# A gated recurrence over 16 batches on one core: one batch a pass, and two

## The chip, the core and the metric

The kernel runs on one NeuronCore of a Trainium2 chip. Times are device microseconds (us) of one execution. The engines are PE (TensorE, matmuls), DVE (VectorE), ACT (ScalarE), POOL (GpSimd) and SP (SyncE, which here only issues transfers). A semaphore is what one engine counts up and another waits for.

## What is computed

`x` is 16 x 224 x 512: 16 batches of 224 tokens. Three stages follow each other, each with a residual and a layer norm: self-attention, cross-attention against a 750-token context, and a recurrent block. Only the last one changes. In the kernel's terms its reference is:

```python
def step(c, xt):                       # scanned over the 16 batches, state c is 224 x 512
    ft = sigmoid(xt @ wf.T + c @ uf.T + bf)
    it = sigmoid(xt @ wi.T + c @ ui.T + bi)
    gt = tanh(xt @ wc.T + c @ uc.T + bc)
    return ft * c + it * gt
c_final = scan(step, c0, x)            # c0 is in_c, the same row for all 224 tokens
h = tanh(x @ wo.T + c_final @ uo.T + bo)
```

The scan is serial over the batches. The input products `xt @ w` don't depend on the state.

## The kernel before

`decoder` calls `self_attention`, `cross_attention` and `feed_forward`, the last of which calls `recurrence` and `output_gate`. Each of these parts is a block of its own; a barrier of all engines stands between two of them.

In `recurrence` everything is turned: 512 state rows lie as 4 groups of 128 partitions, the 224 tokens are the columns. Each f32 operand is split into a rounded part and a rest (`_hi`, `_lo`), and a product is three matmuls: hi x hi, lo x hi, hi x lo. With 4 groups of contraction, one output tile (128 rows x 224 columns) costs 12 matmuls.

- PE: `x_turn(b)` turns batch b with 8 transposes into `ps_x`; `x_part(b)` is the input product, 3 gates x 4 row groups = 12 tiles, 144 matmuls of 224 columns into `ps_gate`, where the sums stay open; `c_part(b)` adds the state product, 144 matmuls more, and closes them. `step(b)` is x_part(b), x_turn(b+1), c_part(b). The six banks of `ps_gate` hold one gate of one half (two row groups) each.
- ACT: `xth` rounds the turned x to `xt_hi`; `gates` takes the tanh of each tile straight from `ps_gate` with the bias (a sigmoid is a tanh of half the argument).
- DVE: `xtl` makes `xt_lo`; `state` combines the gates to the new `c` in halves and splits it into `c_hi` and `c_lo`. `cl_done` is what c_part waits for.
- SP: `load(b)` brings x of the next batch, one buffer `x2_raw`. Ahead of that loop SP loads the recurrence's own weights: three (`wf`, `wi`, `wc`) have come into the three `raw` buffers during cross-attention, then `uf`, `ui`, `uc`, `uo`, `wo` follow, each as soon as its buffer has been split. All of a transfer's descriptors are taken in the order of issue.
- The weights' rounding is ACT's and their rest DVE's; `uo` and `wo` (needed only in `output_gate`) are both POOL's.

While the next state is worked out from batch b's gates, PE does x_part(b+1), which needs no state.

## Time and profile before

| | us |
|---|---|
| median of 3 runs (lowest, highest) | 1599.73 (1598.21, 1603.63) |
| the profiled execution: its time, its span | 1605.2, 1603.3 |
| recurrence, from its first product to its last matmul's start group | 935.54 to 1469.21 |
| one step in the steady loop | 33.0 |
| output gate, to the end | 1474.7 to 1603.3 |

The profile's page gives busy time by engine and in 40 equal slices; the granted PE clock stands in tenths of full speed. Matmuls overlap in the pipeline, so the duration of one (275 ns) is not what it costs: the cost is the distance between the starts of neighbours, called the pitch below. Rows of one kind that follow each other are merged in the timeline, with their count (x4).

### The profile page before, as it was taken

Reading aid. Unit: us, or ns where it says so; the run is one execution under the profiler, and the core shown is the slowest. Engines: PE = TensorE matmul, PEld = TensorE weight load, DVE = VectorE, ACT = ScalarE, POOL = GpSimd, SP = SyncE. Lnnn points to the kernel's source line nnn. Section 1 sums busy time; section 2 is a strip of 40 time slices with the busy share of each in tenths; the row PEclk is TensorE's granted clock in tenths of the full one; section 3 lists DMA queues with packets and bytes.
Section 4 is the critical chain, followed back from the end, with each engine's and each line's share of the span. In section 5 each row is a group of like instructions: output and inputs, shape, how many; then the busy total and the mean of one; then the engine's idle time right before and its main releaser. Section 6 shows DMA issues by size and latency. Waiting matters only on the chain. (4 is left out here: it accounts for less than half of the span.)

```text
span 1603.3 us, 32782 instructions
## 1 busy us (share of the span) xinstructions
PE 1515.5 (95%) x12306; PEld 1342.6 (84%) x12306; DVE 807.8 (50%) x1841; ACT 607.4 (38%) x1883; POOL 530.6 (33%) x398
## 2 busy tenths in 40 slices
PE   6999999996899999999999769999999999998996
PEld 3677777774698999999999669999999999998774
DVE  3688888884255666657566342221222212221676
ACT  4777777771244444444444131111111112211221
POOL 2455454542345666656656221000000000000344
PEclk8899999998899999999999879999999999999998
DMA  2253233222336433434433050000000000001343
GB/s 75 59 170 93 84 87 92 78 62 80 111 110 197 148 122 129 161 119 132 147 130 119 12 175 15 11 11 11 23 11 11 11 11 23 11 0 42 102 138 92
DMA packets 70089, 129.03 MB, mean 80 GB/s; under 512 B 6610, under 2 KB 14802, under 8 KB 70036
## 3 DMA queue, kind: packets, MB, share of 16 engines
q1 hardware_dynamic: 70036, 128.33, 25.5%
q8 instruction: 32, 0.52, 0.1%
q14 instruction: 21, 0.17, 0.0%
HBM read 106.30 MB, written 22.02 MB: 80 GB/s over the span
## 5 line engine op out<-in xcount | busy, mean ns | idle before, releaser
L333 ACT ACTIVATE a_p<-a_ps_s,a_nmax 112x224 f32<-112x224 f32 (+1 forms) x512 | 198.3, 416 | 85.8 <-DVE a_nmax L396 85.8
L510 POOL TENSOR_TENSOR a_p<-a_p,a_rinv 112x896 f32<-112x896 f32 (+1 forms) x128 | 164.8, 1308 | 163.4 <-DVE a_rinv L404 158.7
L1543 POOL MEMSET o_mhalf<- 112x2 f32 x1 | 0.1, 99 | 508.3 <-POOLq L1078 508.3
L1241 ACT ACTIVATE f_gate<-f_ps_gate,f_bias 128x224 f32<-128x224 f32 x192 | 75.4, 444 | 195.2 <-PE f_ps_gate L1204 195.2
L1033 POOL TENSOR_TENSOR x_cx_lo<-x_cx_raw,x_cx_hi 125x512 fp32r<-125x512 f32 x96 | 120.5, 1293 | 83.8 <-ACT x_cx_hi L845 83.8
L1027 POOL TENSOR_TENSOR x_ct_lo<-x_ct_raw,x_ct_hi 128x750 fp32r<-128x750 f32 x64 | 117.5, 1865 | 21.3 <-ACT x_ct_hi L819 21.3
L237 PEld LDWEIGHTS a_ps_t<-a_identity,a_p 112*112 112x112 f32 x768 | 88.2, 137 | 32.1 <-POOL a_p L510 10.3
L333 ACT ACTIVATION_READ_ACCUMULATOR a_p<-a_ps_s,a_nmax 112x1 f32 x512 | 113.7, 222 | 0.0
L237 PE MATMUL a_ps_t<-a_identity,a_p 112*112 112x112 f32 x768 | 109.0, 267 | 2.3 <-DVE a_pt L411 2.2
L1275 DVE TENSOR_TENSOR f_xt_lo<-f_ps_x,f_xt_hi 128x448 fp32r<-128x448 f32 x16 | 10.0, 624 | 195.6 <-ACT f_xt_hi L1232 195.6
L395 DVE TENSOR_REDUCE a_nmax<-a_ps_s 112x1 f32<-112x224 f32 x256 | 97.4, 380 | 19.4 <-PE a_ps_s L224 19.2
L411 DVE COPY a_pt<-a_ps_t 112x448 f32<-112x448 f32 x128 | 79.2, 619 | 46.5 <-PE a_ps_t L237 46.5
L1231 ACT ACTIVATE f_xt_hi<-f_ps_x 128x448 fp32r<-128x448 f32 x16 | 8.7, 543 | 235.1 <-PE f_ps_x L1170 235.1
L1286 DVE SCALAR_TENSOR_TENSOR f_fresh<-f_gate 128x448 f32<-128x448 f32 x32 | 20.0, 625 | 146.8 <-ACT f_gate L1241 146.8
L1020 POOL TENSOR_TENSOR x_x1b<-x_x_raw,x_bv_all 112x1024 f32<-112x1024 f32 x16 | 38.3, 2392 | 94.2 <-DVE x_r L948 92.6
L396 DVE TENSOR_REDUCE a_nmax<-a_ps_s 112x1 f32<-112x112 f32 x256 | 67.5, 264 | 0.0
L266 PE MATMUL a_ps_w<-a_w_hi,a_yt_lo 128*112 128x512 f32 x128 | 64.4, 517 | 0.0
L936 DVE TENSOR_REDUCE x_smax<-x_ps_s 112x1 f32<-112x750 f32 x32 | 30.1, 939 | 58.0 <-PE x_ps_s L762 58.0
L748 PE MATMUL x_ps_g<-x_pt_hi,x_cx_hi 125*128 125x224 f32 x384 | 54.8, 280 | 3.2 <-DVE x_pt_lo L914 3.2
L852 ACT ACTIVATE x_p<-x_ps_s,x_shift 112x750 f32<-112x750 f32 x32 | 28.4, 887 | 75.8 <-DVE x_shift L941 75.8
L748 PE MATMUL x_ps_g<-x_pt_hi,x_cx_lo 125*128 125x224 f32 x384 | 54.2, 278 | 0.0
L218 PE MATMUL a_ps_s<-a_xt,a_zs 32*112 32x224 f32 x512 | 51.1, 399 | 3.2 <-DVE a_bu_split L454 2.1
(225 smaller groups left out, 4046.9 us busy)
## 6 DMA issues: line engine op xcount, KB each, us to landing
x_ct_raw<-in_ct SPq DMA_DIRECT2D x16, 1500.0 KB, 7.8
x_cx_raw<-in_cx SPq DMA_DIRECT2D x16, 1500.0 KB
a_xt<-in_xt SPq DMA_DIRECT2D x16, 448.0 KB, 3.9
a_xrow<-in_x SPq DMA_DIRECT2D x16, 448.0 KB, 3.5
a_xres<-in_x SPq DMA_DIRECT2D x16, 448.0 KB, 4.6
x_scratch<-a_xn SPq DMA_DIRECT2D x16, 448.0 KB, 3.2
x_x_raw<-x_scratch SPq DMA_DIRECT2D x16, 448.0 KB, 3.7
x_scratch<-x_xn SPq DMA_DIRECT2D x16, 448.0 KB, 6.2
```

The source lines that it names most:

```text
L218: pe.matmul(ps_s[0:R, h, 0:T], zs[rows, g, R:T], xt[rows, odd, g, :], start=True, stop=False, skip_group_check=True)
L237: mm = pe.transpose(ps_t[0:R, (g + unit) % 2, h * R:h * R + R], src, identity[0:R, 0:R])
L266: mm = pe.matmul(ps_w[0:R, :], *products[i], start=(i == 0), stop=(i == len(products) - 1))
L333: e = act.activation((p1 if c else p0)[:, g, h, :], src, ACT.Exp, bias=nmax[:, g % 2, c, h:h + 1], accum_out=rsum[:, g % 2, c, h:h + 1])
L395: dve.tensor_reduce(nmax[:, g % 2, 1, h:h + 1], ps_s[0:R, h, 0:T], AX.X, ALU.max, negate=True)
L396: dve.tensor_reduce(nmax[:, g % 2, 0, h:h + 1], ps_s[0:R, h, T:T + R], AX.X, ALU.max, negate=True)\
L411: dve.tensor_copy(transposed(g, unit), unit_bank(g, unit)).then_inc(ptd_done, 1)
L510: pool.tensor_tensor(p[:, g, :, :], p[:, g, :, :], inv, ALU.mult).then_inc(norm_done, 1)
L748: mm = pe.matmul(pair(ps_g, dk), v[:, j, 128 * dk:128 * dk + 128], q[:, j, :], start=(i == 0), stop=(i == 3 * XC - 1))
L1027: pool.tensor_tensor(ct_lo[:, k, 0:TX], ct_raw[:, k, :], ct_hi[:, k, 0:TX], ALU.subtract).then_inc(ctl_done, 1)
L1033: pool.tensor_tensor(cx_lo[:, j, :], cx_raw[:, j, :], cx_hi[:, j, :], ALU.subtract).then_inc(cxl_done, 1)
L1241: a = act.activation(gate[:, j, m, :], region(3 * half + j, k2), ACT.Tanh, bias=bias[:, j, m:m + 1], scale=0.5 if j < 2 else 1.0)
```

## The change

Batches are taken in pairs (8 of them). x of both batches of a pair is turned into `xt_hi`/`xt_lo` of 2 x 224 columns, and `x_part(pair, half)` makes 6 of the pair's 12 tiles with 448 columns in one matmul. A tile goes through `ps_x` (two banks in turn); ACT copies it with the bias into SBUF (`xg_early`, `xg_late`), counted by `xg_done`. The state's two parts stand side by side in `cc`, so `c_tile` has 4 matmuls of hi weights over 448 columns (hi x hi and hi x lo at once) and 4 of lo weights over 224. Nothing is summed in PSUM across these: DVE's new `add` takes the first 224 columns plus the stored input product, then the second 224, per gate and half; ACT's tanh then reads `gate` in SBUF, 448 elements at once.

For batch 0 the state is the same column for all tokens: `u_part` multiplies it as one column with the unsplit weights (48 matmuls) in place of 144, and `opening_gates` feeds the result in as a bias. The state is kept doubled, which saves DVE one operation per half. PE's order is now, for a pair: state product of the first batch (with the two turns of the next pair inside), first half of the next pair's input product, state product of the second batch, second half of the input product. In the last pair there is no next input product; the second batch's first half is done in two pieces by contraction group.

POOL splits `wi` and `ui` at the start. `uo` and `wo` now land in the SBUF of `wf` and `wi`: POOL splits them when the last input product is done. SP loads them into `raw` only after `u_done`, since `u_part` reads `raw`; the loads of x for batches 2 and 3 are issued behind them.

```diff
+            load(0, 0)
+            load(1, 1)
...
             for i in range(3, len(plan)):
-                sp.wait_ge(w_split, i - 2)
+                sp.wait_ge(w_split[i - 3], 1)
+                if i >= 6:
+                    sp.wait_ge(u_done, 1)
                 load_weight(sp, raw[i % 3], raw_in[i % 3], plan[i][0])
-            with sp.Fori(1, B) as b:
-                load(b)
+            with sp.Fori(1, B // 2) as i:
+                for a in range(2):
+                    load(2 * i + a, a)
...
+            def split(i):
...
+            split(1)
+            split(4)
+            pool.wait_ge(xpart_done, TILES * (B // 2))
+            split(6)
+            split(7)
...
+            def x_turn(b, a):
+                if not within(b, B):
+                    return
+                wait(pe, x2_in[a], 8 * (b - a) + 16)
+                if a == 0:
+                    wait(pe, xg_done, (TILES // 2) * b)
+                elif not (isinstance(b, int) and b == 1):
+                    wait(pe, xtl_done, b)
...
+            def x_part(pair, half):
...
+                wait(pe, xtl_done, 2 * pair + 2)
...
+                    for k2 in range(HC):
+                        t = 6 * half + 2 * j + k2
+                        m = slice(128 * (HC * half + k2), 128 * (HC * half + k2) + 128)
+                        if t >= 2:
+                            wait(pe, xg_done, TILES * pair + t - 1)
+                        i = 0
+                        for wp, xp in ((0, xt_hi), (1, xt_hi), (0, xt_lo)):
+                            for k in range(KC):
+                                mm = pe.matmul(ps_x[:, t % 2, 0:2 * T], w["w" + n][wp][:, k, m], xp[:, k, :, :],
+                                               start=(i == 0), stop=(i == 3 * KC - 1))
+                                i += 1
+                        mm.then_inc(xpart_done, 1)
+            def u_part():
+                pe.wait_ge(b_in, 64)
+                for j in range(3):
+                    pe.wait_ge(raw_in[j], 16 * 3)
+                    for m in range(KC):
+                        for k in range(KC):
+                            mm = pe.matmul(ps_gate[:, U_BANK, KC * j + m:KC * j + m + 1], raw[j][:, k, 128 * m:128 * m + 128], c0[:, k:k + 1],
+                                           start=(k == 0), stop=(k == KC - 1))
+                mm.then_inc(u_done, 1)
+            def c_tile(half, j, k2, ks):
+                m = slice(128 * (HC * half + k2), 128 * (HC * half + k2) + 128)
+                hi, lo = w["u" + GATES[j]]
+                for k in ks:
+                    pe.matmul(ps_gate[:, 2 * j + k2, 0:2 * T], hi[:, k, m], cc[:, k, :, :], start=(k == 0), stop=False, skip_group_check=True)
+                for k in ks:
+                    mm = pe.matmul(ps_gate[:, 2 * j + k2, 0:T], lo[:, k, m], cc[:, k, 0, :], start=False, stop=(k == KC - 1),
+                                   skip_group_check=True)
+                return mm
+            def c_gate(b, half, j, ks=range(KC)):
+                if ks[0] == 0:
+                    if isinstance(b, int) and b == 1 and half == 0:
+                        pe.wait_ge(w_split[3 + j], 1)
+                        pe.wait_ge(u_bias_done, 3)
+                    wait(pe, add_done, 6 * (b - 1) + 3 * half + j - 2)
+                for k2 in range(HC):
+                    mm = c_tile(half, j, k2, ks)
+                if ks[-1] == KC - 1:
+                    mm.then_inc(gate_done, 1)
+            def pair_steps(i):
...
+                if not (isinstance(i, int) and i == 0):
+                    wait(pe, cl_done, 2 * first)
+                    c_gate(first, 0, 0)
+                x_turn(first + 2, 0)
+                if not (isinstance(i, int) and i == 0):
+                    c_gate(first, 0, 1)
+                    c_gate(first, 0, 2)
+                x_turn(first + 3, 1)
+                if not (isinstance(i, int) and i == 0):
+                    for j in range(3):
+                        c_gate(first, 1, j)
+                x_part(i + 1, 0)
+                if isinstance(i, int) and i == B // 2 - 1:
+                    pe.wait_ge(cl_done, 2 * second - 1)
+                    for j in range(3):
+                        c_gate(second, 0, j, range(0, HC))
+                    pe.wait_ge(cl_done, 2 * second)
+                    for j in range(3):
+                        c_gate(second, 0, j, range(HC, KC))
+                else:
+                    wait(pe, cl_done, 2 * second)
+                    for j in range(3):
+                        c_gate(second, 0, j)
+                for j in range(3):
+                    c_gate(second, 1, j)
+                x_part(i + 1, 1)
+            x_turn(0, 0)
+            x_turn(1, 1)
+            for half in range(2):
+                x_part(0, half)
+            u_part()
+            pair_steps(0)
+            with pe.Fori(1, B // 2 - 2) as i:
+                pair_steps(i)
+            for i in range(B // 2 - 2, B // 2):
+                pair_steps(i)
...
+                wait(act, xpart_done, (TILES // 2) * (b - a))
+                act.activation(xt_hi[:, 0:2, a, :], turned(b, 0), ACT.Copy)
+                act.activation(xt_hi[:, 2:4, a, :], turned(b, 2), ACT.Copy).then_inc(xth_done, 1)
...
+            def opening_gates():
+                act.wait_ge(u_done, 1)
+                for j in range(3):
+                    act.activation(u_bias[:, j, :], ps_gate[:, U_BANK, KC * j:KC * j + KC], ACT.Copy, scale=0.5 if j < 2 else 1.0)\
+                       .then_inc(u_bias_done, 1)
+                act.wait_ge(u_bias_done, 3)
+                act.wait_ge(xg_done, TILES)
                 for half in range(2):
...
-                            a = act.activation(gate[:, j, m, :], region(3 * half + j, k2), ACT.Tanh, bias=bias[:, j, m:m + 1],
+                            a = act.activation(gate[:, j, m, :], pre(0, half, j)[:, k2, 0, :], ACT.Tanh, bias=u_bias[:, j, m:m + 1],
                                                scale=0.5 if j < 2 else 1.0)
                         a.then_inc(act_done, 1)
...
+            def pair_steps(i, odd_pair):
+                if isinstance(i, int) and i == 0:
+                    xth(2, 0)
+                    opening_gates()
+                    xth(3, 1)
+                else:
+                    xth(2 * i + 2, 0)
+                    gate_tanh(2 * i, 0, 0)
+                    gate_tanh(2 * i, 0, 1)
+                    xth(2 * i + 3, 1)
+                    gate_tanh(2 * i, 0, 2)
+                    for j in range(3):
+                        gate_tanh(2 * i, 1, j)
+                x_gates(i + 1, 1 - odd_pair, 0)
+                for half in range(2):
+                    for j in range(3):
+                        gate_tanh(2 * i + 1, half, j)
+                x_gates(i + 1, 1 - odd_pair, 1)
...
+            round_weight(0)
+            xth(0, 0)
+            xth(1, 1)
+            round_weight(2)
+            act.wait_ge(b_in, 64)
+            for j in range(3):
+                x_gate(0, 0, 0, j)
+                if j == 1:
+                    round_weight(3)
+            for j in range(3):
+                x_gate(0, 0, 1, j)
+                if j == 1:
+                    round_weight(5)
+            for i in range(2):
+                pair_steps(i, i)
+            with act.Fori(1, B // 4 - 1) as i:
+                for odd_pair in range(2):
+                    pair_steps(2 * i + odd_pair, odd_pair)
+            for i in range(B // 2 - 2, B // 2):
+                pair_steps(i, i % 2)
...
+            def add(b, odd_pair, a, half, j):
+                cols = slice(HC * half, HC * half + HC)
+                n = 6 * (b - 1) + 3 * half + j
+                wait(dve, gate_done, n + 1)
+                wait(dve, xg_done, 6 * (b - a) + 6 * half + 2 * j + 2)
+                dve.tensor_tensor(gate[:, j, cols, :], ps_gate[:, 2 * j:2 * j + 2, 0:T], pre(odd_pair, half, j)[:, :, a, :],
+                                  ALU.add).then_inc(hi_added, 1)
+                wait(dve, hi_added, n + 1)
+                dve.tensor_tensor(gate[:, j, cols, :], ps_gate[:, 2 * j:2 * j + 2, T:2 * T], gate[:, j, cols, :],
+                                  ALU.add).then_inc(add_done, 1)
...
+                dve.scalar_tensor_tensor(out=state[:, cols, :], in0=kept[:, cols, :], scalar=0.5, in1=fresh[:, cols, :],
+                                         op0=ALU.mult, op1=ALU.add).then_inc(state_done, 1)
...
+                dve.tensor_scalar(cc[:, cols, 0, :], state[:, cols, :], 0.5, None, ALU.mult).then_inc(ch_done, 1)
+                wait(dve, ch_done, n + 1)
+                dve.scalar_tensor_tensor(out=cc[:, cols, 1, :], in0=state[:, cols, :], scalar=0.5, in1=cc[:, cols, 0, :],
+                                         op0=ALU.mult, op1=ALU.subtract).then_inc(cl_done, 1)
+            def second_half(b, odd_pair, a):
+                add(b, odd_pair, a, 1, 0)
+                add(b, odd_pair, a, 1, 1)
+                split(b, 0)
+                add(b, odd_pair, a, 1, 2)
+                cell(b, 1)
+                split(b, 1)
+            def pair_steps(i, odd_pair):
+                if isinstance(i, int) and i == 0:
+                    xtl(2, 0)
+                    cell(0, 0)
+                    split(0, 0)
+                    cell(0, 1)
+                    split(0, 1)
+                    xtl(3, 1)
+                else:
+                    add(2 * i, odd_pair, 0, 0, 0)
+                    xtl(2 * i + 2, 0)
+                    add(2 * i, odd_pair, 0, 0, 1)
+                    add(2 * i, odd_pair, 0, 0, 2)
+                    xtl(2 * i + 3, 1)
+                    cell(2 * i, 0)
+                    second_half(2 * i, odd_pair, 0)
+                for j in range(3):
+                    add(2 * i + 1, odd_pair, 1, 0, j)
+                cell(2 * i + 1, 0)
+                second_half(2 * i + 1, odd_pair, 1)
```

PE in the steady loop of the kernel before, at the seam between the input product of one batch and its state product (the stationary operand is named last):

```order
L1187 MATMUL f_ps_gate<-f_xt_hi,f_wc_hi 128x224 x4
L1187 MATMUL f_ps_gate<-f_xt_hi,f_wc_lo 128x224 x4
L1187 MATMUL f_ps_gate<-f_xt_lo,f_wc_hi 128x224 x4
L1170 MATMUL f_ps_x<-f_identity,f_x_raw 128x112 x8
L1204 MATMUL f_ps_gate<-f_c_hi,f_uf_hi 128x224 x4
L1204 MATMUL f_ps_gate<-f_c_hi,f_uf_lo 128x224 x4
L1204 MATMUL f_ps_gate<-f_c_lo,f_uf_hi 128x224 x4
```

PE in the kernel after, at the top of a pair, where the turn stands between two gates of the first batch's state product:

```order
L1238 MATMUL f_ps_gate<-f_cc,f_uf_hi 128x448 x4
L1240 MATMUL f_ps_gate<-f_cc,f_uf_lo 128x224 x4
L37 ISA
L37 REGISTER_ALU
L1201 MATMUL f_ps_x<-f_identity,f_x_raw 128x112 x8
L37 REGISTER_ALU
L1238 MATMUL f_ps_gate<-f_cc,f_ui_hi 128x448 x4
L1240 MATMUL f_ps_gate<-f_cc,f_ui_lo 128x224 x4
```

Three groups of four matmuls of 224 columns per tile have become one group of four with 448 columns and one with 224.

The second place is the start of the recurrence after the first pair's input product. SP's queue there, before:

```order
L46 DMA w_raw<-in_uf_t 128x4x512 [waits f_w_split]
L46 DMA w_raw<-in_ui_t 128x4x512 [waits f_w_split]
L46 DMA w_raw<-in_uc_t 128x4x512 [waits f_w_split]
L46 DMA w_raw<-in_uo_t 128x4x512 [waits f_w_split]
L46 DMA w_raw<-in_wo_t 128x4x512 [waits f_w_split]
L1143 UNCONDITIONAL_BRANCH
L1132 ISA [waits f_xt_done]
L1132 DMA f_x_raw<-x_scratch 112x2x512
```

and after:

```order
L46 DMA w_raw<-in_uf_t 128x4x512 [waits f_w0_split]
L46 DMA w_raw<-in_ui_t 128x4x512 [waits f_w1_split]
L46 DMA w_raw<-in_uc_t 128x4x512 [waits f_w2_split]
L46 DMA w_raw<-in_uo_t 128x4x512 [waits f_u_done,f_w3_split]
L46 DMA w_raw<-in_wo_t 128x4x512 [waits f_u_done,f_w4_split]
L1162 UNCONDITIONAL_BRANCH
L1162 ISA
L1149 ISA [waits f_xt_done]
L1149 DMA f_x_raw<-x_scratch 112x2x512
```

The loads of `uo`, `wo` and x now stand behind PE's `u_part`. The third place is ACT after the first pair's last input tile, in the kernel after:

```order
L1302 ACTIVATE f_xt_hi<-f_ps_x 128x2x224 [waits f_xpart_done,f_xt_done]
L1303 ACTIVATE f_xt_hi<-f_ps_x 128x2x224
L1328 ACTIVATE f_u_bias<-f_ps_gate 128x4 [waits f_u_done]
L1328 ACTIVATE f_u_bias<-f_ps_gate 128x4 x2
L1336 ACTIVATE f_gate<-f_xg_early,f_u_bias 128x224 [waits f_xg_done,f_u_bias_done]
L1336 ACTIVATE f_gate<-f_xg_early,f_u_bias 128x224 x5
L1336 ACTIVATE f_gate<-f_xg_late,f_u_bias 128x224 x6
L1302 ACTIVATE f_xt_hi<-f_ps_x 128x2x224 [waits f_xpart_done,f_xt_done]
```

The rounding of batch 2's turned x stands ahead of batch 0's gates, that of batch 3 behind them.

## Rows read from the trace of the kernel before

**Rows 1.** The page: PE's busy share and granted clock in 40 equal slices.
```profile
PE   6999999996899999999999769999999999998996
PEclk8899999998899999999999879999999999999998
```

**Rows 2.** Windows: us, then busy (instructions) by engine, clock, DMA share.
```profile
1092.00:1422.00 330.00, 330.00 (x2969) 330.00 (x2967) 75.53 (x140) 57.21 (x141) 0.00 (x0) 1.00 0.05 14
```

**Rows 3.** Timeline, PE, one input product, the turn: start, us, line, tile.
```profile
1075.19 0.61 PE L1187 MATMUL f_ps_gate<-f_xt_hi,f_wf_hi 128*128 128x224 f32 x4
...
1091.27 0.93 PE L1170 MATMUL f_ps_x<-f_identity,f_x_raw 112*128 112x112 f32 x8
...
1091.97 0.69 PE L1204 MATMUL f_ps_gate<-f_c_hi,f_uf_hi 128*128 128x224 f32 x4
```

**Rows 4.** Timeline, PE in cross-attention, 376 and 512 columns.
```profile
704.11 1.52 PE L762 MATMUL x_ps_s<-x_ct_hi,x_zt_hi 128*112 128x376 f32 x8
...
712.31 0.93 PE L716 MATMUL x_ps_g<-x_identity,x_x_raw 112*128 112x112 f32 x8
...
713.99 1.08 PE L774 MATMUL x_ps_h<-x_wv_lo,x_ot_hi 128*112 128x512 f32 x4
...
717.69 1.09 PE L774 MATMUL x_ps_h<-x_wv_hi,x_ot_lo 128*112 128x512 f32 x4
```

**Rows 5.** By line: a product of one column with unsplit weights.
```profile
L703 PEld LDWEIGHTS x_ps_g<-x_bq,w_raw x32: 191/192/193, 413.1 to 416.8; 128*128 128x128 f32 x32
```

**Rows 6.** Timeline, opening of the recurrence, all engines.
```profile
929.03 1.73 PE L1170 MATMUL f_ps_x<-f_identity,f_x_raw 112*128 112x112 f32 x8 [12.15 <-DMA f_x_raw<-x_scratch]
...
935.54 1.20 PE L1187 MATMUL f_ps_gate<-f_xt_hi,f_wf_hi 128*128 128x224 f32 x4 [4.78 <-DVE f_xt_lo L1276]
940.80 0.71 PE L1187 MATMUL f_ps_gate<-f_xt_hi,f_wi_hi 128*128 128x224 f32 x4
...
947.85 0.37 SPq L46 DMA_DIRECT2D w_raw<-in_wo_t  x1
...
957.83 1.57 PE L1170 MATMUL f_ps_x<-f_identity,f_x_raw 112*128 112x112 f32 x8 [3.36 <-DMA f_x_raw<-x_scratch]
```

**Rows 7.** DMA view: transfers, KB each, us from issue to landing.
```profile
w_raw<-in_uf_t SPq DMA_DIRECT2D x1, 1024.0 KB, 5.2
...
w_raw<-in_wo_t SPq DMA_DIRECT2D x1, 1024.0 KB, 8.8
```

**Rows 8.** By tile, the recurrence's x: shortest, median, longest landing.
```profile
DMA to landing us min/median/max: 3.4/3.6/9.3
```

**Rows 9.** Timeline, POOL's split of `wo` and a DVE operation beside it.
```profile
959.79 1.89 POOL L1157 CAST f_wo_hi<-w_raw 128x2048 fp32r<-128x2048 f32 x1
...
961.76 4.58 POOL L1159 TENSOR_TENSOR f_wo_lo<-w_raw,f_wo_hi 128x2048 fp32r<-128x2048 f32 x1
...
964.00 2.82 DVE L1283 SCALAR_TENSOR_TENSOR f_keep<-f_gate,f_c 128x448 f32<-128x448 f32 x1 [2.39 <-ACT f_gate L1241]
```

**Rows 10.** Timeline, the last matmuls of the recurrence and the state's last steps.
```profile
1469.21 0.61 PE L1204 MATMUL f_ps_gate<-f_c_lo,f_uc_hi 128*128 128x224 f32 x4
1469.85 0.78 ACT L1241 ACTIVATE f_gate<-f_ps_gate,f_bias 128x224 f32<-128x224 f32 x2 [1.90 <-PE f_ps_gate L1204]
1470.67 0.62 DVE L1286 SCALAR_TENSOR_TENSOR f_fresh<-f_gate 128x448 f32<-128x448 f32 x1 [4.73 <-ACT f_gate L1241]
...
1473.33 0.39 DVE L1298 CAST f_c_hi<-f_c 128x448 fp32r<-128x448 f32 x1
1473.75 0.62 DVE L1300 TENSOR_TENSOR f_c_lo<-f_c,f_c_hi 128x448 fp32r<-128x448 f32 x1
```

**Rows 11.** By line: a DVE sum from two banks; `xtl`; ACT's rounding.
```profile
L1496 DVE TENSOR_TENSOR o_pre<-o_ps_o,o_base x16: 1217/1224/1226, 1492.0 to 1591.3; 112x1024 f32<-112x1024 f32 x16
...
L1275 DVE TENSOR_TENSOR f_xt_lo<-f_ps_x,f_xt_hi x16: 618/625/625, 934.3 to 1422.7; 128x448 fp32r<-128x448 f32 x16
...
L1231 ACT ACTIVATE f_xt_hi<-f_ps_x 128x448 fp32r<-128x448 f32 x16 | 8.7, 543 | 235.1 <-PE f_ps_x L1170 235.1
```

More of the change, by code:

```diff
@@ L1209, in step @@
-            def step(b, more=True):
-                x_part(b)
-                if more:
-                    x_turn(b + 1)
-                c_part(b)
-            x_turn(0)
-            step(0)
-            with pe.Fori(1, B - 1) as b:
-                step(b)
-            step(B - 1, more=False)
+            def x_part(pair, half):
+                if not within(pair, B // 2):
+                    return
+                wait(pe, xtl_done, 2 * pair + 2)
+                for j, n in enumerate(GATES):
+                    if isinstance(pair, int) and pair == 0 and half == 0:
+                        pe.wait_ge(w_split[j], 1)
+                    for k2 in range(HC):
[10 more added lines that the diff above has]
+                        mm.then_inc(xpart_done, 1)
@@ new lines, in x_gate, with x_gates @@
+            def x_gate(pair, odd_pair, half, j):
+                for k2 in range(HC):
+                    t = 6 * half + 2 * j + k2
+                    m = HC * half + k2
+                    wait(act, xpart_done, TILES * pair + t + 1)
+                    act.activation(pre(odd_pair, half, j)[:, k2, :, :], ps_x[:, t % 2, 0:2 * T].rearrange("p (a t) -> p a t", a=2),
+                                   ACT.Identity, bias=bias[:, j, m:m + 1]).then_inc(xg_done, 1)
+            def x_gates(pair, odd_pair, half):
+                if not within(pair, B // 2):
+                    return
+                wait(act, add_done, 6 * (2 * pair - 1) if half else 6 * (2 * pair - 3))
+                for j in range(3):
+                    x_gate(pair, odd_pair, half, j)
@@ new lines, in gate_tanh @@
+            def gate_tanh(b, half, j):
+                cols = slice(HC * half, HC * half + HC)
+                wait(act, add_done, 6 * (b - 1) + 3 * half + j + 1)
+                act.activation(gate[:, j, cols, :], gate[:, j, cols, :], ACT.Tanh, scale=0.5 if j < 2 else 1.0).then_inc(act_done, 1)
+            def opening_gates():
[5 more added lines that the diff above has]
+                act.wait_ge(xg_done, TILES)
@@ L1242, in gates @@
                                                scale=0.5 if j < 2 else 1.0)
                         a.then_inc(act_done, 1)
-            def step(b, more=True):
-                if more:
-                    xth(b + 1)
-                gates(b)
-            for i in range(6):
-                act.wait_ge(raw_in[i % 3], 16 * (i // 3 + 2))
-                act.activation(plan[i][1][:], raw[i % 3][:], ACT.Copy).then_inc(w_rounded, 1)
-                if i == 0:
-                    xth(0)
-            step(0)
@@ L1302, in step @@
-            def step(b, more=True):
-                if more:
-                    xtl(b + 1)
-                state(b)
-            for i in range(6):
-                dve.wait_ge(w_rounded, i + 1)
-                dve.tensor_tensor(plan[i][2][:], raw[i % 3][:], plan[i][1][:], ALU.subtract).then_inc(w_split, 1)
-                if i == 0:
-                    xtl(0)
-                if i == 1:
-                    start()
-            step(0)
-            with dve.Fori(1, B - 1) as b:
-                step(b)
@@ new lines, in split_weight @@
+            def split_weight(i):
+                dve.wait_ge(w_rounded[i], 1)
+                dve.tensor_tensor(plan[i][2][:], raw[i % 3][:], plan[i][1][:], ALU.subtract).then_inc(w_split[i], 1)
+            split_weight(0)
+            xtl(0, 0)
+            xtl(1, 1)
+            split_weight(2)
+            start()
+            split_weight(3)
+            split_weight(5)
+            for i in range(2):
+                pair_steps(i, i)
+            with dve.Fori(1, B // 4 - 1) as i:
+                for odd_pair in range(2):
+                    pair_steps(2 * i + odd_pair, odd_pair)
```

198 lines of the change are left out of this document (79 added, 119 removed).

## The prediction, as made before the changed kernel had run

> **What bounds the kernel now.** I read the slices first, then the window of the steady loop, then the timeline inside one step, and last the two ends of the recurrence. The slices [rows 1] show PE at nine tenths or more from the 25th to the 36th slice, at the full granted clock; that is the stage the change touches. The window [rows 2] says it sharply: in ten steps (330.0 us, 33.0 each) PE is busy for all 330.0 us, DVE for 75.5, ACT for 57.2. No wait of PE is left in the loop, so only less PE work can shorten it, and a new wait of PE costs its full length.
>
> PE work must be counted by pitch. One input product of 144 matmuls of 224 columns runs from 1075.19 to 1091.27 [rows 3]: 16.08 us, 0.1117 us each. The turn takes 0.70. A step is 288 x 0.1117 + 0.70 = 32.9, which leaves about 0.15 for the seams: it closes on 33.0. Wider matmuls stand in cross-attention [rows 4]: 48 of 376 columns in 8.20 us, 0.171 each, and 16 of 512 columns in 3.70 us, 0.2313 each. From 224 to 512 columns the pitch grows by 0.1196 us, 0.415 ns a column, which is the 2.4 GHz level; what is left over, 18 to 19 ns, comes with every matmul whatever its width.
>
> **Term A, the matmuls.** A line from 224 to 512 gives 0.2047 us for 448 columns, one from 376 to 512 gives 0.2029. No row has the rounded type, 448 columns and 128 weight columns together (the wide rows load 112); if the 18 ns grew with the weights, 128/112, the pitch would be 0.2075. I take 0.205, the row of 512 being nearest. Before: 16 batches x 288 = 4608 x 0.1117 = 514.7. After: input products 8 pairs x 12 tiles x 12 = 1152 of 448 columns; state products 15 batches x 12 tiles x 4 = 720 of 448 and 720 of 224. 1872 x 0.205 + 720 x 0.1117 = 383.8 + 80.4 = 464.2. **-50.5 us**, of which 13.4 is batch 0's missing state product at 144 x 224 columns and the rest is the leftover of 2016 instructions. Ends: -54 and -46.
>
> The Trainium skill (TensorE: Matmul & The Clock Gate, Back-to-back issue gap) puts the warm gap at N/2.4 plus 2.5 ns. By it the 2016 instructions fewer would be worth 5 us, not 37, and term A would be -18. The rows show 18 ns at both 224 and 512 columns, so the trace disagrees, and the measured pitches stand.
>
> **Term B, the one-column product.** 32 such matmuls start within 413.1 to 416.8 [rows 5], 0.119 us each. 48 x 0.119 = **+5.7**; PE is alone with it, nothing hides it.
>
> **Term C, the opening.** Before, x of batch 1 was issued right after the last weight (947.85), landed in the 9.3 us of [rows 8], and PE waited 3.36 us for it at 957.83 [rows 6]. Now `uo` and `wo` wait for `u_done`, and x of batches 2 and 3 stand behind both in SP's queue. Call the end of `u_part` U. A lone weight lands in 5.2 us [rows 7]; before, the second of two close ones came about 3.5 us after the first, and x 1.2 behind it (947.85 + 8.8 = 956.65, PE starts at 957.83). So x of batch 2 lands at U + 10.7 with a little for issuing. Then, with PE idle: turn at half clock 1.7 [rows 6], `xth` 1.1 [rows 11], the three small bias copies about 0.7 (estimate from ACT's shortest operations), and 12 tanh of 224 elements, at the 0.35 to 0.4 us apart that two in 0.78 us mean [rows 10]. ACT is done at about U + 18.7. DVE cannot keep up: cell and split of a half are 3 x 0.62 + 0.39 + 0.62 with gaps [rows 10], about 3.1; the first half's end at U + 19.1, the second's at 22.2, and `xtl` of batch 3, 1.2 [rows 11], ends at U + 23.5. Only then may PE begin the next input product. Two turns (1.4) are in this and counted elsewhere: +22.1, less the old wait 3.4: **+18.7**. Ends: if x overtook the weights and landed in the median 3.6 [rows 8], 6 us less; if the two weights share more badly or POOL and DVE get in each other's way at the start (see F), 2 to 4 more.
>
> **Term D, clock.** After the gap at the barrier the first products run at half clock until about 940.8, 5.3 us [rows 6], worth 2.5; before, the 3.4 us wait cost some 1.5 more. Now there is the same first stretch and, after 23 us of near idleness, a second full one: 4.9 against 4.0, **+0.9**. One turn fewer stands inside PE's stretch (batch 1's is ahead of it, hidden in ACT's and DVE's work; start stays near 935.5): **-0.8**.
>
> **Term E, the steady pairs.** PE has 144 x 0.205 + 2 x (48 x 0.205 + 48 x 0.1117) + 1.7 for turns and seams = 61.6 us a pair, against 66.0. What must hide under it: a gate takes PE 2.53 us; DVE's two sums of it take 2 x 0.62 + 0.1. The two-bank reading has its row: 1024 elements from two banks in 1.22 us [rows 11], so 448 are not dearer than the 0.62 of `xtl`. From the last matmul of a batch: sums 1.35, tanh 0.55, fresh, state, split: 4.5 us, while PE has 14.8 us of input product. A tile of it is 2.46 us; PE needs the tile two back copied by ACT (0.54). ACT is held by the last tanh until about 2.4, and PE would stall only from 4.9. DVE has in the first batch of a pair 12 sums, 4 `xtl`, 2 cells and splits, some 16.5 us inside about 20. **0**, with 2 us of slack a place. The tail after the last matmul was 4.5 us (1469.85 to 1474.37) and stays: two sums more, a tanh of 448 for two of 224, one operation less, and one split instead of two.
>
> **Term F, the last pair.** No input product lies between batches 14 and 15. PE has the first piece of batch 15, half of three gates, 3.8 us, against 4.6 to cl_done: a stall of 1. But POOL begins its 13 us of splits exactly there, when the last input product is done. [Rows 9] show a DVE operation with both inputs in SBUF taking 2.82 us instead of 0.62, and ending 0.5 after POOL's subtraction (961.76 + 4.58). POOL's second subtraction would stand from about 8.8 to 13.3 us into the pair; cell(14, 0) is due at 9.1. Shifted to 13.3, the chain ends at 23.6 instead of 19.9: stall **+4.7**, with 1 as the low end.
>
> **The sum.** -50.5 + 5.7 + 18.7 + 0.9 - 0.8 + 4.7 = -21.3 us. Profiled execution: 1605.2 - 21.3 = 1583.9. That execution lies 5.5 above the median of the runs; the difference carries over: 1599.7 - 21.3 = **1578.4**.
>
> **Rivals.**
> 1. *x is not held up behind the weights.* The DMA rows give 3.6 for a lone x, 9.3 only behind weights. If it lands by U + 4.6, C is 6 less: 1572. Against it: the 9.3 itself was one x behind two weights.
> 2. *The leftover goes with the columns, not with the instruction.* Then 448 columns cost 2 x 0.1117 = 0.2234, A is only -16, and the kernel ends 13 us slower: 1613. It decides from a pitch of 0.216. Against it stand the 0.171 of 376 and 0.2313 of 512 columns; for it, that none of these rows has 128 weight columns. The skill's small fixed part, beside term A, is the same thought: little to gain from fewer instructions.
> 3. *DVE becomes the bound.* Should a sum take 1.05 us instead of 0.62 (PE writing neighbouring banks meanwhile, which no row shows with DVE reading two), DVE falls behind by 10 x 0.43 in a batch, 2 us of slack are gone, and PE loses about 3 us a pair: break-even; at 1.25 us about 5.5 x 7 = 38, hence 1617.
> 4. *The opening is masked or POOL's lock misses the cells*: F at 1 and C somewhat less: 1574. It lies in the forecast's own range.
>
> **How the numbers follow.** Forecast with its own bounds (A 203 to 207.5 ns, C -3 to +4, F 1 to 5): 0.76, 1570 to 1588. Rival 1: 0.10, 1568 to 1574. Rival 2: 0.03. Rival 3: 0.05, spread over 1590 to 1620. An equal time from several small stalls: 0.03; the remaining 0.03 goes to an unseen gain. Range 1567 to 1589 for 8 in 10. A measurement of this kernel can tell 0.3% (5 us) from no change. Faster 0.89, within 0.04, slower 0.07.
>
> **What would show it.** Steady pair of 61.6 us with PE busy throughout: A and E; 144 matmuls of 448 columns in 29.5 us: A alone. A PE wait for x of batch 2 of 9 to 12 us after `u_part`, then one of about 11 us that DVE's `xtl` ends: C. A PE wait of 4 to 5 us at batch 15 with a cell operation of several us beside POOL: F. PE waiting on `xg_done` or `add_done` in the loop would be rival 3 and would make the prediction wrong; so would a pitch near 0.22.

## The result and the profile after

| | before | after |
|---|---|---|
| median of the runs | 1599.73 us (1598.21 to 1603.63, 5 runs) | 1592.78 us (1587.89 to 1596.05, 5 runs) |
| ratio, with its 95% interval | | 0.9945 (0.9919 to 0.9971) |
| profiled execution | 1605.2 us, span 1603.3 | 1596.05 us, span 1594.2 |

The kernel became faster by about half a per cent, 7 us, where 21 were forecast; the time lies above the forecast range (1567 to 1589). The two profiled executions differ by 9.1 us of span. In the stage itself, from the first input product to the issue end of the last matmul, before took 534.1 us (935.54 to 1469.66) and after 523.15 (936.11 to 1459.26): 11.0 us less. The other 1.9 us were lost in the tail (0.9), in the output stage (0.4) and ahead of the stage (0.6). Since the start of the first input product wanders from 930.1 to 936.1 between executions of all the kernels below, the readings compare stretches within the stage and not whole spans. The profiled executions also lie at different distances above their medians, 5.5 us before and 3.3 after: the stage's 11.0 us less, minus 1.9 lost around it, minus these 2.2, are the 7 us of the medians.

The slices of the page after, to set beside [rows 1]. The 24th to 26th slice (917 to 1036 us) hold the start of the stage and its opening, and the clock stands at seven tenths in all three; before, the dip was two slices long. The 37th slice (1435 to 1475 us) holds the last pair, where PE and its clock now dip too:

```profile
PE   6999999996899999999999867799999999997996
...
PEclk7899999998899999999999977799999999998998
```

Windows of after: us, then busy (instructions) of PE, PEld, DVE, ACT and POOL, clock, DMA share. The first is the steady loop, as [rows 2]; the others go through the opening in order.

```profile
1060.00:1368.00 308.00, 308.00 (x1770) 288.00 (x1769) 141.08 (x243) 80.41 (x140) 0.00 (x0) 1.00 0.05 15
...
971.00:972.00 1.00, 1.00 (x12) 1.00 (x11) 0.00 (x0) 0.00 (x0) 0.00 (x0) 1.00 0.00 0
...
974.00:985.00 11.00, 10.99 (x52) 10.90 (x52) 0.00 (x0) 0.00 (x0) 0.00 (x0) 0.50 0.00 0
...
985.00:1008.00 23.00, 3.96 (x17) 3.30 (x18) 7.76 (x14) 6.61 (x19) 0.00 (x0) 0.50 0.58 171
1008.00:1040.00 32.00, 32.00 (x166) 29.63 (x166) 7.94 (x13) 6.71 (x11) 0.00 (x0) 0.91 0.01 1
```

In the loop PE is busy for 308.0 of 308.0 us at the full clock, while DVE does 141.1. One pair, read between two turns (1063.33 and 1124.66), takes 61.33 us; two steps of before took 65.88. The loop therefore did what it should. Everything else happened at the ends.

The timeline of after, PE: four matmuls of 448 columns in the first input product, then the opening, with ACT's last gates of batch 0 and DVE's `xtl` of batch 3. They answer to [rows 4] and [rows 6].

```profile
943.74 0.98 PE L1219 MATMUL f_ps_x<-f_xt_hi,f_wi_hi 128*128 128x448 f32 x4
944.56 0.99 PE L1219 MATMUL f_ps_x<-f_xt_hi,f_wi_lo 128*128 128x448 f32 x4
...
968.38 16.61 PE L1230 MATMUL f_ps_gate<-f_c,w_raw 128*128 128x1 f32 x96
...
995.69 1.75 PE L1201 MATMUL f_ps_x<-f_identity,f_x_raw 112*128 112x112 f32 x8 [10.70 <-DMA f_x_raw<-x_scratch]
...
999.79 1.73 PE L1201 MATMUL f_ps_x<-f_identity,f_x_raw 112*128 112x112 f32 x8 [2.35 <-DVE f_xt_lo L1399]
...
1000.94 2.33 ACT L1336 ACTIVATE f_gate<-f_xg_late,f_u_bias 128x224 f32<-128x224 f32 x6
...
1006.32 1.15 DVE L1399 TENSOR_TENSOR f_xt_lo<-f_ps_x,f_xt_hi 128x448 fp32r<-128x448 f32 x2
...
1007.52 1.86 PE L1219 MATMUL f_ps_x<-f_xt_hi,f_wf_hi 128*128 128x448 f32 x4 [6.00 <-DVE f_xt_lo L1399]
```

The groups of four start 0.82 us apart: 0.205 us for 448 columns. The one-column product takes 16.61 us and has 96 records, though the program issues 48 such matmuls. It ends at 984.99, and the next input product begins 22.5 us later. The records of that line, durations in ns (least, median, most):

```profile
L1230 PEld LDWEIGHTS f_ps_gate<-f_c,w_raw x96: 188/333/333, 968.2 to 984.6; 128*128 128x128 f32 x96
L1230 PE MATMUL f_ps_gate<-f_c,w_raw x96: 167/352/353, 968.4 to 984.6; 128*128 128x1 f32 x96
```

The least weight load is about that of [rows 5] (191 there), the median 1.8 times it: most of the stretch ran at half clock, as the windows show (1.00 up to 972, 0.50 from 973 on).

The timeline of after in the last pair, POOL and DVE, PE's wait, and the first matmuls of the second piece; then a window of PE's first piece:

```profile
1429.78 1.91 POOL L1177 CAST f_wi_hi<-w_raw 128x2048 fp32r<-128x2048 f32 x1
...
1431.77 4.61 POOL L1179 TENSOR_TENSOR f_wi_lo<-w_raw,f_wi_hi 128x2048 fp32r<-128x2048 f32 x1
1431.96 4.90 DVE L1417 SCALAR_TENSOR_TENSOR f_kept<-f_gate,f_state 128x448 f32<-128x448 f32 x1
...
1441.52 1.11 PE L1238 MATMUL f_ps_gate<-f_cc,f_uf_hi 128*128 128x448 f32 x2 [3.24 <-DVE f_cc L1434]
...
1447.96 0.57 PE L1238 MATMUL f_ps_gate<-f_cc,f_uf_hi 128*128 128x448 f32 x2
```

```profile
1441.00:1447.00 6.00, 5.48 (x18) 5.09 (x19) 4.43 (x8) 0.70 (x2) 0.00 (x0) 0.50 0.00 0
```

DVE's `kept` of batch 14 should take 0.62 us. It starts 0.19 us after the start of POOL's subtraction and ends 0.48 after its end; the operation in [rows 9] also ended 0.48 after POOL's. PE's first piece of batch 15 (1441.52 to 1447.96) then runs almost wholly at half clock.

The end of the stage, DVE's operations after the last matmul (issue end 1459.26), to set beside [rows 10]:

```profile
1459.52 0.39 DVE L1432 TENSOR_SCALAR f_cc<-f_state 128x448 fp32r<-128x448 f32 x1 [1.31 <-PE f_ps_gate L1240]
1459.95 0.62 DVE L1434 SCALAR_TENSOR_TENSOR f_cc<-f_state,f_cc 128x448 fp32r<-128x448 f32 x1
1460.49 0.62 DVE L1407 TENSOR_TENSOR f_gate<-f_ps_gate,f_xg_late 128x448 f32<-128x448 f32 x1
...
1465.18 2.02 PE L1565 MATMUL o_ps_o<-f_wf_hi,f_cc 128*112 128x512 f32 x4 [5.77 <-PEq L1078]
```

The first half's split waits for the last matmul, although that half's state was ready long before: `cc` is still being read until then (`gate_done`). It stands ahead of the last gate's two sums in DVE's order.

### The profile page after: what moved, and what is told of

It is laid out like the page before. It is cut to its first block and busy times, and to the rows that moved or that the text cites. A ratio compares the mean times of both kernels' runs of the same rounds, so it can differ in the third digit from the quotient of the medians.

```text
span 1594.2 us, 29003 instructions
## 1 busy us (share of the span) xinstructions
PE 1489.7 (93%) x10386; PEld 1282.7 (80%) x10386; DVE 901.3 (57%) x1985; ACT 643.5 (40%) x1888; POOL 545.7 (34%) x402
## 5 line engine op out<-in xcount | busy, mean ns | idle before, releaser
L1407 DVE TENSOR_TENSOR f_gate<-f_ps_gate,f_xg_early 128x448 f32<-128x448 f32 x45 | 28.1, 625 | 208.3 <-PE f_ps_gate L1240 208.3
L1323 ACT ACTIVATE f_gate<-f_gate 128x448 f32<-128x448 f32 x90 | 52.1, 579 | 187.3 <-DVE f_gate L1410 187.3
L1310 ACT ACTIVATE f_xg_early<-f_ps_x,f_bias 128x448 f32<-128x448 f32 x48 | 30.4, 634 | 82.9 <-PE f_ps_x L1219 82.9
L1238 PE MATMUL f_ps_gate<-f_cc,f_uf_hi 128*128 128x448 f32 x240 | 60.6, 373 | 3.2 <-DVE f_cc L1434 3.2
L1238 PE MATMUL f_ps_gate<-f_cc,f_ui_hi 128*128 128x448 f32 x240 | 60.6, 373 | 0.0
L1238 PE MATMUL f_ps_gate<-f_cc,f_uc_hi 128*128 128x448 f32 x240 | 59.8, 370 | 0.0
L1310 ACT ACTIVATE f_xg_late<-f_ps_x,f_bias 128x448 f32<-128x448 f32 x48 | 30.4, 633 | 70.7 <-PE f_ps_x L1219 70.7
```

Of the source, the lines that this page charges most:

```text
L1238: pe.matmul(ps_gate[:, 2 * j + k2, 0:2 * T], hi[:, k, m], cc[:, k, :, :], start=(k == 0), stop=False, skip_group_check=True)
L1310: act.activation(pre(odd_pair, half, j)[:, k2, :, :], ps_x[:, t % 2, 0:2 * T].rearrange("p (a t) -> p a t", a=2), ACT.Identity, bias=bias[ ...
L1323: act.activation(gate[:, j, cols, :], gate[:, j, cols, :], ACT.Tanh, scale=0.5 if j < 2 else 1.0).then_inc(act_done, 1)
```

## The experiments

Eight kernels were run beside the kernel before, whose median there was 1600.5 us for e1, e5, e2 and e3 and 1600.1 for the rest; the ratio of after is to 1599.7. The medians are of 2 runs for e1, e5, e2 and e4, of 4 for e3, 8 for e6 and 5 for e8. The stretches are read from the profiled executions. "Opening" is from the first input product to the second pair's, "pairs" the six after it up to the start of the last pair, "end" from there to the first matmul of the output stage.

| kernel | median, us | ratio (95%) | opening | pairs | end |
|---|---|---|---|---|---|
| after | 1592.8 | 0.9945 (0.9919 to 0.9971) | 71.4 | 415.5 | 42.2 |
| e1_few_u | 1576.6 | 0.9853 (0.9820 to 0.9886) | 57.0 | 414.4 | 41.2 |
| e5_spread_u | 1584.7 | 0.9904 (0.9869 to 0.9938) | 65.1 | 415.5 | 42.1 |
| e2_x_first | 1578.6 | 0.9865 (0.9832 to 0.9899) | 60.6 | 414.2 | 41.2 |
| e3_step0_full | 1565.7 | 0.9782 (0.9758 to 0.9805) | 49.0 | 412.7 | 41.2 |
| e4_pool_pieces | 1586.7 | 0.9916 (0.9891 to 0.9941) | 70.8 | 415.6 | 38.1 |
| e7_no_late_split | 1589.1 (one run) | | 71.0 | 415.4 | 38.1 |
| e6_three_passes | 1598.7 | 0.9992 (0.9981 to 1.0004) | 70.7 | 427.1 | 38.9 |
| e8_best | 1560.6 | 0.9756 (0.9738 to 0.9774) | 48.8 | 412.7 | 38.1 |

My theory after the result: the loop earned what was forecast, and the loss sits in the opening, where the one-column product costs 16.6 us and the chain behind it 22.5. The rival was that the loss is spread over the pairs (DVE's two sums, contention), with the opening hidden by something else.

The spans that the expectations name were worked out from the profiled execution of after, the slowest of its five runs. The measured spans lie 4 to 10 us below them, and 2.4 to 6.0 us of that is only an earlier start of the stage. So each expectation is held against its stretch, not its span. The last column also wanders: it is 42.2 in after and e5 and 41.2 in e1, e2 and e3, with the same wait of 3.24 or 3.25 us in all five. Behind that wait the half clock lasts longer in the first two: the first piece of batch 15 takes 6.4 us in after and 5.4 in e1.

### Is the one-column product's own work the price?

`u_part` with the first of its four row blocks only, so 12 matmuls for 48; three quarters of batch 0's state product are left out.

```diff
-                        for k in range(KC):
+                        for k in range(1):
                             mm = pe.matmul(ps_gate[:, U_BANK, ...
-                                           start=(k == 0), stop=(k == KC - 1))
+                                           start=True, stop=True)
```

> The one-column product keeps only one of the four contraction groups for each of its 12 output columns: 12 matmuls instead of 48, and batch 0's state product is incomplete. In the trace of after the 48 matmuls are 96 records and take 16.6 us, while the granted clock falls. Theory (each unsplit f32 matmul is two passes, and the clock falls in the long one-column stretch): 24 records at the full-clock spacing of 0.119 us, 2.9 us, so the stretch gets 13.7 us shorter and the span about 1580.5. Rival (the stretch is long because of something fixed, such as waiting for the weights or for b_in): it stays near 16 us and the span near 1594.

The timeline of this kernel:

```profile
963.98 2.73 PE L1230 MATMUL f_ps_gate<-f_c,w_raw 128*128 128x1 f32 x24
...
976.78 1.76 PE L1201 MATMUL f_ps_x<-f_identity,f_x_raw 112*128 112x112 f32 x8 [10.07 <-DMA f_x_raw<-x_scratch]
```

Twelve matmuls leave 24 records in 2.73 us, 0.23 us a matmul at the full clock. The opening is 14.4 us shorter, 13.9 of it in this stretch, and the kernel 16 us faster in the medians. Behind it the waits are the same, 10.07 us for x among them, so nothing that was hidden by the product comes to light.

### How much of it is the clock?

The same 48 matmuls, eight behind each of the last six tiles of the first input product instead of all in a row (`u_part` now takes the tile's number and does its eight).

```diff
                         mm.then_inc(xpart_done, 1)
+                        if isinstance(pair, int) and pair == 0 and half == 1:
+                            u_part(t - 6)
...
-            u_part()
             pair_steps(0)
```

> The 48 one-column matmuls are spread in groups of 8 behind the six tiles of the first pair's second half of the input product. Theory (half of their time is the clock, which falls when PE does nothing but one-column matmuls): among wide matmuls the clock stays full, their 96 passes cost about 11.4 us together instead of 16.6, the recurrence is 5 us shorter, span about 1589. Rival (a pass of unsplit f32 with 128 weight columns costs 0.17 us at any clock): no change, 1594.

The timeline of this kernel, and a window of it:

```profile
957.78 1.84 PE L1234 MATMUL f_ps_gate<-f_c,w_raw 128*128 128x1 f32 x16
959.48 1.06 PE L1219 MATMUL f_ps_x<-f_xt_hi,f_wi_hi 128*128 128x448 f32 x4
```

```profile
955.00:977.00 22.00, 21.61 (x144) 20.49 (x143) 2.29 (x1) 4.98 (x6) 0.00 (x0) 1.00 0.00 1
```

Eight matmuls take 1.70 us (957.78 to 959.48), 0.213 each, so 48 take 10.2 us, and the clock stays at 1.00. In a row they took 16.6, so 6.4 us of that are the clock's: 30 of the 48 matmuls at twice 0.213 make the difference. From the start of the first input product to the end of the last one-column matmul the stretch is 5.7 us shorter than in after.

### Is x held up behind the weights?

The x of batches 2 and 3 is issued ahead of the `uo` and `wo` loads.

```diff
             for i in range(3, len(plan)):
+                if i == 6:
+                    load(2, 0)
+                    load(3, 1)
                 sp.wait_ge(w_split[i - 3], 1)
...
-            with sp.Fori(1, B // 2) as i:
+            with sp.Fori(2, B // 2) as i:
```

> SP issues the loads of x for batches 2 and 3 ahead of the loads of uo and wo, nothing else changes. Theory (the wait of 10.7 us after the one-column product is x behind 2 MB of weights): x is there long before, the turn follows u_part at once, and the stretch from its end to the next input product falls from 22.5 to about 12 us; span about 1584. Rival (ACT's and DVE's opening work sets that stretch, x only fills it): it stays above 20 us.

The timeline of this kernel: no wait is left for the first turn, and those on DVE stand as before.

```profile
982.96 1.73 PE L1204 MATMUL f_ps_x<-f_identity,f_x_raw 112*128 112x112 f32 x8 [2.35 <-DVE f_xt_lo L1402]
...
990.69 1.86 PE L1222 MATMUL f_ps_x<-f_xt_hi,f_wf_hi 128*128 128x448 f32 x4 [6.00 <-DVE f_xt_lo L1402]
```

The product ends at 979.0, and the next input product begins 11.7 us later instead of 22.5. The whole 10.7 us wait for x was the order in SP's queue, and it covered nothing.

### What is the whole opening worth?

Batch 0 as an ordinary step: its state product is computed with the split weights, the state is split once at the start, and the one-column product, its bias copies and SP's wait for it are gone.

```diff
                     sp.wait_ge(w_split[i - 3], 1)
-                if i >= 6:
-                    sp.wait_ge(u_done, 1)
...
-            u_part()
             pair_steps(0)
...
-                if not (isinstance(i, int) and i == 0):
-                    wait(pe, cl_done, 2 * first)
-                    c_gate(first, 0, 0)
+                wait(pe, cl_done, 2 * first + 2)
+                c_gate(first, 0, 0)
                 x_turn(first + 2, 0)
```

> Everything of the change except its third part: batch 0 goes through the ordinary 48 + 48 matmuls a step, with the state split at the start, no one-column product, no separate opening on ACT and DVE, uo and wo loaded as soon as their buffers are split. Theory (the one-column product costs more than it saves, since it is serial and leaves PE idle behind it): it removes 16.6 us of product, 22.5 us to the next input product and 2.5 us of half clock, and adds 15.2 us of matmuls and 1.4 us of turns that now are hidden between: 25 us less than after, span about 1569, ratio to before about 0.979. Rival (the stretch behind it is the pair scheme's own: the next pair's x must be turned and split before PE can go on): a stall of 10 us or more stays in the first pair and the span is 1580 or more.

Timeline and a window of this kernel: the state product follows the input product, and the next input product follows that.

```profile
966.08 0.98 PE L1236 MATMUL f_ps_gate<-f_cc,f_uf_hi 128*128 128x448 f32 x4
...
982.72 0.99 PE L1217 MATMUL f_ps_x<-f_xt_hi,f_wf_hi 128*128 128x448 f32 x4
```

```profile
960.00:985.00 25.00, 25.00 (x155) 23.57 (x154) 14.30 (x22) 8.34 (x13) 0.00 (x0) 1.00 0.21 57
```

The state product and both turns take 16.6 us at the full clock, 22.4 less than `u_part` and the chain behind it together. The pairs behind are 2.8 us shorter too: in after they begin at half clock after the idle opening. That makes 25.2 us: so much the edit "state product of the first step as one column" cost net. The 1.0 us at the end is not in it, since e1 and e2 show it with the one-column product in place. Without that edit the change is worth 35 us (ratio 0.9782) and not 7.

### Is it POOL that delays the last pair?

First the subtractions of POOL's splits in four pieces of 512 elements.

```diff
-                pool.tensor_tensor(lo[:], raw[i % 3][:], hi[:], ALU.subtract).then_inc(w_split[i], 1)
+                for k in range(KC):
+                    p = pool.tensor_tensor(lo[:, k, :], raw[i % 3][:, k, :], hi[:, k, :], ALU.subtract)
+                p.then_inc(w_split[i], 1)
```

> POOL's four subtractions of 128x2048 are each cut into four of 128x512; nothing else changes. Theory (DVE's cell in the last pair stood 4.9 us behind one POOL subtraction, which holds a shared resource for one instruction): the operation waits at most about 1.2 us a piece, PE's wait at batch 15 falls from 3.4 to about 1.5 us, the clock doesn't fall there, and the last pair, 36.2 us in after, is about 32.6. Rival (the wait at batch 15 is that the state's split may not start before the last matmul that reads it; POOL only filled it): 35 us or more.

Then without the two late splits at all; the output gate of this kernel takes `wf` and `wi` in place of `uo` and `wo`, so its output is not the reference's.

```diff
-            pool.wait_ge(xpart_done, TILES * (B // 2))
-            split(6)
-            split(7)
```

> POOL's split of uo and wo at the last pair is left out, so the output gate works with the weights wf and wi in their place. It gives the last pair without POOL: theory 32.6 us (stall about 1.2 us for the split of the first half, then about 1.2 us more at the second piece), rival 35 us or more, as for the run in pieces.

The timeline of the kernel with pieces:

```profile
1429.69 6.08 POOL L1180 TENSOR_TENSOR f_wi_lo<-w_raw,f_wi_hi 128x512 fp32r<-128x512 f32 x4
1430.16 1.56 DVE L1422 SCALAR_TENSOR_TENSOR f_fresh<-f_gate 128x448 f32<-128x448 f32 x1
1431.83 1.53 DVE L1426 SCALAR_TENSOR_TENSOR f_state<-f_kept,f_fresh 128x448 f32<-128x448 f32 x1
...
1436.97 0.67 PE L1240 MATMUL f_ps_gate<-f_cc,f_uf_hi 128*128 128x448 f32 x2 [1.22 <-DVE f_cc L1436]
...
1441.25 0.68 PE L1240 MATMUL f_ps_gate<-f_cc,f_uf_hi 128*128 128x448 f32 x2 [0.27 <-DVE f_cc L1436]
```

DVE now gets in between two pieces: 1.56 us at most instead of 4.90, for 1.5 us more of POOL (6.08 for 4.61). The end is 4.1 us shorter than in after (3.1 shorter than in e1, e2 and e3), and exactly as long as without POOL, 38.10 in both. So these 3 to 4 us come from POOL's long subtraction: 1.8 us of the 4.1 is less waiting, and the rest is the half clock behind the wait, for with the pieces the granted clock stays at 1.00 there. Waits of 1.22 and about 0.27 us stay without POOL. PE is idle from 1435.75, its last matmul of batch 14, to 1436.97, and in between DVE does the first half's split, which had to wait for that matmul.

### Does the loop's gain come from the wider matmul?

The state product with three groups of 224 columns into one sum, and one sum on DVE, while all else is as in after (the cut shows PE's part only).

```diff
                 for k in ks:
-                    pe.matmul(ps_gate[:, 2 * j + k2, 0:2 * T], hi[:, k, m], cc[:, k, :, :], ...
+            for a in range(2):
+                for k in ks:
+                    pe.matmul(ps_gate[:, 2 * j + k2, 0:T], hi[:, k, m], cc[:, k, a, :], ...
```

> The state product goes back to three groups of four matmuls of 224 columns into one sum, and DVE to one addition a gate; the input product by pairs in SBUF stays. Theory (every matmul carries about 18 ns whatever its width): 15 x 12 x 4 pairs of 0.111 us in place of one of 0.205, 720 x 0.017 = 12 us more on PE, steady pair 63.2 instead of 61.6 us, span about 1606. Rival (the 448-column form costs what two of 224 cost, or DVE's second addition is on the path): pair at 61.6 us or less.

The median is 5.9 us above that of after, at equality with before. The six pairs take 11.6 us more, 1.95 a pair: turns stand 63.28 apart (1121.11 to 1184.39) instead of 61.33. The expectation had 96 x (2 x 0.1117 - 0.205) = 1.8 from 96 instructions more. With the 0.1097 us that the 224-column matmuls take in after between those of 448, 24 tiles x (12 x 0.1117 - 4 x 0.2053 - 4 x 0.1097) give 1.9. PE's own work thus accounts for the pair in both kernels, and no DVE time is on PE's path.

The span was expected at about 1606 and was 1596.2: the stage began 5.2 us earlier than in after, and the end is 3.3 us shorter. The timeline of this kernel, its last pair:

```profile
1438.23 4.82 DVE L1419 SCALAR_TENSOR_TENSOR f_fresh<-f_gate 128x448 f32<-128x448 f32 x1
...
1446.18 0.70 PE L1239 MATMUL f_ps_gate<-f_cc,f_uf_hi 128*128 128x224 f32 x4 [1.22 <-DVE f_cc L1433]
```

DVE is held for 4.82 us here too, yet PE waits only 1.22 us, as without POOL. By the trace, the sum less per gate lets DVE catch up before the last matmul of batch 14, for which the split waits; no run tests this alone.

### Both ends mended

The ordinary first step, x ahead of the weights, and the pieces, together.

> Batch 0 through the ordinary step (as in the run without the one-column product), x of batches 2 and 3 loaded ahead of uo and wo, POOL's subtractions in four pieces. Theory: 25 us from the opening and 3 to 4 us from the last pair: span about 1565, ratio to before about 0.977. Rival (POOL's pieces or the first pair's turns leave stalls): 1570 or more.

Median 1560.6 us (5 runs), ratio 0.9756 (0.9738 to 0.9774): 39.5 us faster than before and 32 faster than the change. With an ordinary first step x ahead of the weights gains nothing measurable more (opening 48.8 for 49.0), since PE did not wait for it; the pieces bring 3.1 us at the end.

## Why the prediction was wrong

The forecast was -21.3 us in the stage, and it measured -11.0. Term by term, where A is the matmul counts at the pitches read in after (0.2053 and 0.1097 us), and F the last pair's 36.25 us less 30.2 for its 24 tiles at those pitches:

| term | forecast | measured |
|---|---|---|
| A, matmuls | -50.5 | -51.4 |
| B, one-column product | +5.7 | +16.6 |
| C, opening behind it | +18.7 | +17.7 |
| D, clock | +0.9 - 0.8 | not read apart; the sum closes with it as forecast |
| E, steady pairs: stalls | 0 | 0 |
| F, last pair | +4.7 | +6.05 |
| tail | 0 | +0.9 (behind the stage) |

**B is the step that failed:** +5.7 us for 48 one-column matmuls at 0.119 us each, where 16.6 were measured. Its 10.9 us are the whole error of 10.3 in the stage; that the other terms cancel to within 0.6 (A -0.9, C -1.0, F +1.35) is luck. It has two parts. The first is a misread count. [Rows 5] show 32 records, and I called them "32 such matmuls". There were 16: an unsplit f32 product leaves two records an instruction, as the 96 records of 48 matmuls and the 24 of 12 show. 48 x 0.213 = 10.2, which is 4.5 more than 48 x 0.119. The program's own count (4 x 4 products in that line) stood beside the row and would have told it. The second part is the clock, 6.4 us, and term D gave that stretch no clock risk at all. PE was busy for 10.99 of 11.00 us and still ran at the 1.2 GHz level, from 973 to the end of the product. Spread among wide matmuls, the same work kept 1.00. A row of 3.7 us [rows 5] could not show what 10 us of it would do; the price needed an upper end at twice the pitch, some 20 us, and the range a higher end with it.

**C was right step by step.** x landed 10.70 us after the product's end (forecast 10.7). That match is closer than the working: its parts, 5.2 + 3.5 + 1.2, make 9.9, and the rest was "a little for issuing"; in the five other kernels with the same order the wait was 10.0 to 10.3. ACT finished the gates at 18.3 (18.7), and DVE's `xtl` ended at 22.5 (23.5), all counted from the product's end. Rival 1, x not held up, fell: the wait went only when the order in SP's queue was changed.

**A and E were right**, and with them rivals 2 and 3 fell. The pitch is 0.205 us for 448 columns with 128 weight columns, so the leftover of 18 to 19 ns goes with the instruction. "Whatever its width" was too strong: the 376-column row of the forecast leaves only about 15 ns, and the 224-column matmuls between those of 448 about 17 (0.1097 us). A steady pair took 61.33 for 61.6. DVE's sum of two banks took 0.62 us while PE wrote the neighbouring ones.

**D held where it could be read.** The second stretch at half clock after the idle opening cost 2.8 us (415.5 against 412.7 for the same six pairs with an ordinary first step), where 2.5 were in the forecast. The same six pairs took 414.2 to 415.6 in the other kernels with an idle opening and the same loop, so this cost is 1.5 to 2.9 from one execution to the next.

**F had the right cause and was too small by 1.35.** One operation with both inputs in SBUF began 0.19 us after POOL's second subtraction and was held for its whole length, 4.90 us. The Trainium skill (SBUF — State Buffer, SBUF: two separate sides) tells of a port pair that DVE and POOL share under an exclusive lock; this trace agrees, with 4.90 us for an operation of 0.62 beside one of POOL of 4.61. What the step left out came behind the stall: PE ran on at 0.50 until 1447, so the pieces that should fill 3.8 us took 6.4. The stall itself was 3.24, not 4.7. It also left out that the first half's split cannot start before the batch's last matmul; most of the 1.5 us that stay without POOL is that wait, as the timeline of e4 shows, but no run took it away.

**The tail** was called even, by counting operations. It counted one split behind the last matmul. There are two: the first half's, held by `gate_done` until then, stands ahead of the last gate's sums in DVE's order (0.97 us, 1459.52 to 1460.49). This is read from the trace; no run changed it.

The sign was called right, by half the forecast margin in the stage and a third of it in the medians.

## What to carry to other kernels

Count instructions in the program and records in the trace before dividing one by the other: here each unsplit f32 matmul left two. Price a long stretch of narrow matmuls at both clock levels. A step that saves matmul columns at the start of a loop is dear when it breaks the overlap there: a state product and two turns of 16.6 us gave way to 16.6 us of one-column work and 22.5 of chain. Before moving a load behind a new wait, see what stands behind it in the same queue, and cut a long POOL operation into pieces where a dependent DVE chain runs beside it.

## What the runs showed of the hardware

- A stretch in which PE is busy throughout can lose the clock: 16.6 us of one-column f32 matmuls ran at 1.00 up to 972 and at 0.50 from 973 to 985. Groups of 1.7 us of the same matmuls between ones of 448 columns, and a single stretch of 2.7 us, kept 1.00.
- A one-column f32 matmul with 128 weight columns takes 0.21 to 0.23 us at the full clock and 0.42 to 0.43 at half (52 records in the window of 11.0 us), in two records. A rounded one of 448 columns takes 0.205.
- Beside the columns' time (at 0.415 ns a column) about 19 ns come with a rounded matmul of 128 weight columns, at 448 columns (0.2053 us) as at 224 (0.1117). Where the two widths take turns, the 224 take 0.1097, so about 17 are left.
- A DVE operation with two inputs in SBUF that meets a POOL subtraction waits for its end, 4.90 us beside 4.61; with POOL's work in pieces of about 1.5 us it waits for one piece, 1.56.
- The operation that is caught differs: it was `kept` in after (4.90 us) and `fresh` in e6_three_passes (4.82 us). What it costs PE differs too: a wait of 3.24 us in the first and of 1.22 in the second.
